# Where a two-layer transformer kernel splits its expert weights: spread over four stages in place of one

## The reference, cut to what matters

```python
def _attention(h, W_qkv, b_qkv, W_proj, b_proj):
    qkv = h @ W_qkv + b_qkv
    ...
    scores = jnp.einsum('blhd,bmhd->bhlm', q * scale, k)
    attn = jax.nn.softmax(scores, axis=-1)
    o = jnp.einsum('bhlm,bmhd->blhd', attn, v).reshape(b, l, c)
    return o @ W_proj + b_proj
# layer 0
h = _modulate(_layernorm(x), shift_msa, scale_msa)
x = x + gate_msa * _attention(h, W_qkv, b_qkv, W_proj, b_proj)
h = _modulate(_layernorm(x), shift_mlp, scale_mlp)
x = x + gate_mlp * (jax.nn.gelu(h @ W_fc1 + b_fc1, approximate=True) @ W_fc2 + b_fc2)
# layer 1: the same attention, then
gate_logits = xf @ w_gate
topk_logits, topk_idx = jax.lax.top_k(gate_logits, 2)
hmid = jax.nn.gelu(jnp.einsum('tc,ech->eth', xf, w1) + b1[:, None, :], approximate=True)
eo = jnp.einsum('eth,ehc->etc', hmid, w2) + b2[:, None, :]
moe = jnp.einsum('te,etc->tc', cw, eo).reshape(B, N, C)
return x + g_mlp[:, None, :] * moe
```

## Time and profile before

| | us |
|---|---|
| median of three runs | 1630.94 (1626.31 to 1634.62) |
| the profiled execution, its own time | 1625.62 |
| span of its core, first to last instruction | 1623.9 |
| mean granted TensorE clock | 0.922 of full speed |

### The profile page before, as it was taken

One profiled execution on the slowest core, in us unless ns is written; L12 is line 12 of the kernel. 1 busy time (PEld: TensorE's weight loads), 2 busy tenths in 40 slices (PEclk: granted clock), 3 DMA queues, 4 the chain that ended last, 5 costly groups with the idle time before them and its releaser, 6 DMA issues. The chain is left out here.

```text
span 1623.9 us, 25041 instructions
## 1 busy us (share of the span) xinstructions
PE 1400.8 (86%) x8657; PEld 870.6 (54%) x8657; DVE 1092.9 (67%) x1859; ACT 798.2 (49%) x1537; POOL 647.2 (40%) x873
## 2 busy tenths in 40 slices
PE   4787988998899879987789899999977299999995
PEld 2563333333333458976633333333325299999995
DVE  3657878887797254446489889889926556656663
ACT  0441766766677552225327677677763233333331
POOL 0125767767720000001269999995004612112121
PEclk9995989998899989998859999999998599999998
DMA  7275577657720309003660222220019466767673
GB/s 187 63 201 99 137 190 166 179 174 174 178 90 3 136 10 292 1 1 95 187 103 11 47 46 46 46 47 3 3 61 356 145 204 189 238 189 236 187 234 77
DMA packets 93396, 204.22 MB, mean 126 GB/s; under 512 B 35846, under 2 KB 61384, under 8 KB 90028
## 3 DMA queue, kind: packets, MB, share of 16 engines
q1 hardware_dynamic: 59788, 121.26, 23.4%
q0 software_dynamic: 33488, 81.41, 22.5%
HBM read 131.56 MB, written 72.12 MB: 125 GB/s over the span
## 5 line engine op out<-in xcount | busy, mean ns | idle before, releaser
L958 DVE TENSOR_REDUCE att_neg_max<-att_for_max 128x1 f32<-128x1024 f32 x512 | 601.7, 1220 | 106.5 <-PE att_for_max L1033 103.8
L943 ACT ACTIVATE att_probs<-att_scores 128x512 f32<-128x512 f32 x1002 | 523.9, 606 | 262.3 <-PE att_scores L1072 261.8
L1083 PE MATMUL att_out<-att_probs,V 128*32 128x512 f32 x2048 | 283.9, 627 | 3.9 <-ACT att_probs L943 2.0
L1072 PE MATMUL att_scores<-att_QS,att_KS 56*128 56x512 f32 x618 | 235.1, 467 | 38.1 <-DMA att_QS<-att_neg_max_rows 21.2
L1033 PE MATMUL att_for_max<-att_KS,att_QS 54*128 54x512 f32 x640 | 247.8, 474 | 0.7 <-DVE att_neg_max L958 0.5
L1072 PEld LDWEIGHTS att_scores<-att_QS,att_KS 56*128 56x128 f32 x618 | 105.4, 192 | 205.1 <-ACT att_probs L943 140.9
L1033 PE MATMUL att_for_max<-KS,QS 54*128 54x512 f32 x384 | 165.9, 535 | 25.8 <-DVE att_neg_max L958 13.1
L1875 ACT ACTIVATE experts_gelu<-experts_proj,experts_b 128x256 f32<-128x256 f32 x171 | 81.3, 475 | 208.6 <-PE experts_proj L1944 185.4
L1944 PE MATMUL experts_proj<-experts_x_parts,w_parts 128*128 128x256 f32 (+1 forms) x1197 | 174.1, 286 | 1.4 <-DVE experts_x_parts L1669 1.4
L1823 POOL DMA_INDIRECT sums_of_experts<-experts_y,experts_rows x38 | 61.3, 1613 | 260.0 <-DVE experts_y L1705 254.2
L1072 PE MATMUL att_scores<-QS,KS 56*128 56x512 f32 x384 | 150.7, 466 | 12.2 <-ACT att_probs L943 10.7
(11 more groups left out here) (227 smaller groups left out, 2004.9 us busy)
## 6 DMA issues: line engine op xcount, KB each, us to landing
w_parts<-w_parts SPq DMA_DIRECT2D x20, 2304.0 KB, 8.7
w_parts<-att_w_parts POOLq DMA_DIRECT2D x15, 864.0 KB, 5.9
w_parts<-w_parts SPq DMA_DIRECT2D x5, 2592.0 KB, 15.6
qk_halves<-qkv_qk_parts SPq DMA_DIRECT2D x40, 288.0 KB
w_parts<-att_w_parts POOLq DMA_DIRECT2D x20, 576.0 KB, 5.6
slot_rows<-mlp_blank_rows SPq DMA_DIRECT2D x2, 5145.0 KB, 28.2
att_QS<-qk_halves POOLq DMA_DIRECT2D x120, 72.0 KB
att_KS<-qk_halves POOLq DMA_DIRECT2D x60, 144.0 KB
```

What stands on the lines that cost most here:

```text
L943: nc.scalar.activation(PR[st % 2][:, j, :], score_bank(st, n), ACT.Exp, scale=SCALE).then_inc(exp_done, 1)
L958: nc.vector.tensor_reduce(negm[half][:, c:c + 1], psM[ring % 2][:].rearrange("p a n -> p (a n)"), AX_X, ALU.max, negate=True).then_inc(rin ...
L1072: nc.tensor.matmul(score_bank(st, n), KS[g % SLOTS][rows, p, k * P:(k + 1) * P], QS[g % SLOTS][rows, half, p, :], start=True, stop=True).t ...
L1083: last = nc.tensor.matmul(psO[32 * j:32 * j + 32, :], T.V[:, g, k, 32 * j:32 * j + 32], PR[st % 2][:, j, :], start=(k == 0), stop=(k == KT ...
```

## The change

The list of 30 pieces is dealt out: 6 to qkv 0 (3 before POOL's wait for the stores of q and k, 3 behind `load_group`), 8 to attention 0 (one per half of a group, from group 2 on, for four groups), 10 to MLP 0 (one at each 3.6 units), 6 to qkv 1 (as in qkv 0). The code of a piece is the same, moved into a class. In the qkv stages the parts' buffers lie in the unused part of the output tile `heads_out`, and in MLP 0 in buffers of their own. The blank rows leave MLP 0 and are written in attention 1 by POOL's queue, in six shares, one behind each load of a group. `router_rows` moves ahead of the load of group 2.

```diff
+class Splitter:
+    def load(self, pool):
...
+    def split(self, pool):
...
+    def finish(self, pool):
+        for slot, done in enumerate(self.piece_out):
+            if self.outs[slot]:
+                pool.wait_ge(done, 16 * self.outs[slot])
...
 # qkv_stage, POOL
+            S.load(pool)
             v = T.V[:].rearrange("p g k (j d) -> p (g k j) d", j=HG)
...
             pool.wait_ge(v_filled, 4)
+            for _ in range(len(pieces) // 2):
+                S.split(pool)
             for c in range(QK_CHUNKS):
...
             load_group(pool, T, 0, T.QS0, T.KS0, group_in)
+            for _ in range(len(pieces) - len(pieces) // 2):
+                S.split(pool)
+            S.finish(pool)
             pool.wait_ge(group_in, LOADS)
 # attention_stage, POOL
+            def blank_rows(n):
+                rows = T.slots.rearrange("(k t p) r -> t p k r", t=ETILES, p=P)
+                k0, k1 = n * BLOCKS // LATER, (n + 1) * BLOCKS // LATER
+                for t in range(ETILES):
+                    nc.gpsimd.dma_start(rows[t][:, k0:k1, :], blank[:, t:t + 1, :].broadcast_to([P, k1 - k0, ROW])
+                                        ).then_inc(blank_out, 16)
...
             def side_work(g):
-                for n in range((g - SLOTS + 1) * per_group, min((g - SLOTS + 2) * per_group, side)):
-                    if splits:
-                        split_piece(n)
-                    else:
-                        router_columns(n)
+                n = g - SLOTS + 1
+                if pieces:
+                    for half in range(HALVES):
+                        if half:
+                            pool.wait_ge(scores_ready, ((g - SLOTS + 1) * HALVES + half) * KT * HG)
+                        for _ in range(n * HALVES + half, len(pieces), LATER * HALVES):
+                            S.split(pool)
+                    return
+                blank_rows(n)
+                items = TILES + B * GPB
+                for m in range(n * items // LATER, (n + 1) * items // LATER):
+                    router_columns(m)
...
+                if g == 1 and not pieces:
+                    router_rows()
 # mlp_stage
-            sp.wait_ge(blank_ready, 1)
-            for t in range(ETILES):
-                sp.dma_start(T.slots.rearrange("(k t p) r -> t p k r", t=ETILES, p=P)[t],
-                             blank[:, t:t + 1, :].broadcast_to([P, SLOT_ROWS // EBLK, ROW])).then_inc(blank_out, 16)
...
+            S.load(pool)
+            for n in range(len(pieces)):
+                if n:
+                    pool.wait_ge(h_ready, n * NBLK * NF // len(pieces))
+                S.split(pool)
+            S.finish(pool)
 # program
-                qkv_stage(nc, T, l, W)
-                attention_stage(nc, T, l, W, splits if l == 0 else [])
+                qkv_stage(nc, T, l, W, splits[24:30] if l else splits[0:6])
+                attention_stage(nc, T, l, W, [] if l else splits[6:14])
-                mlp_stage(nc, T, l, W, layers[1])
+                mlp_stage(nc, T, l, W, splits[14:24], layers[1])
```

More of the change, by code:

```diff
@@ L488, in qkv_stage @@
         stored = [sem(f"stored{c}") for c in range(QK_CHUNKS)]
-        pieces = [len(chunk_pieces(c)) for c in range(QK_CHUNKS)]
+        stores = [len(chunk_pieces(c)) for c in range(QK_CHUNKS)]
         def hT_of(i):
@@ L533, in _ @@
             for c in range(QK_CHUNKS):
-                act.sem_inc(stored[c], 16 * pieces[c])
+                act.sem_inc(stored[c], 16 * stores[c])
             norm_root(nc, act, N, 0)
@@ L709, in attention_stage @@
         last = sb("last_inverse", [P, BLK], F32)
[L710 to L712 removed]
+        if pieces:
+            S = Splitter(nc, T, pieces, sb("w_f32", [P, FF], F32), [sb(f"w_parts{n}", [P, 2, FF], F32R) for n in range(2)],
+                         sem)
         else:
+            blank = sb("blank_rows", [P, ETILES, ROW], F32)
             wgate = sb("w_gate_rows", [P, C, E], F32)
@@ L925, in _ @@
             pool.wait_ge(wp_gated, B)
-            for n in range(2):
-                if splits:
-                    pool.wait_ge(piece_out[n], 16 * outs[n])
+            if pieces:
+                S.finish(pool)
+            else:
+                pool.wait_ge(blank_out, 16 * (ETILES * LATER + 1))
         @block.scalar
@@ L1237, in mlp_stage @@
         hp = [sb(f"hidden_parts{n}", [P, 2, BLK], F32R) for n in range(RING)]
-        blank = sb("blank_rows", [P, ETILES, ROW], F32)
+        S = Splitter(nc, T, pieces, sb("w_f32", [P, FF], F32), [sb(f"w_parts{n}", [P, 2, FF], F32R) for n in range(2)], sem)
         YB = TPB + 1
```

146 lines of the change are left out of this document (77 added, 69 removed).

## The result

The changed kernel took 1651.5 us (median of 4 runs, 1646.8 to 1656.2) against 1632.5 before: a ratio of 1.0136, interval 1.0102 to 1.0171. It is 1.4% slower; the prediction said 1619 with a range of 1602 to 1638.

What follows compares the result with a forecast made beforehand. Attention 0 was held to lose time as maxima wait behind group loads, then to a lowered clock; MLP 0 PE-bound, qkv a chain over all engines. Terms -30 + 17 + 1 + 0 = -12 gave 1619 us, range 1602 to 1638.

Steps and rivals of the forecast that it cites:

- the two qkv stages: qkv 0 and 1: six pieces each add 8.5 us a stage, 17 for both, bounds 8 and 36.
- The path: qkv stages: three pieces behind the load reach the barrier, next stage at 131.3 against 127.3, +4.0 us.
- The period of 7.44: Time from cast to next cast of a piece, in us, used twice for the pieces behind the qkv load.
- sharing: qkv stages: pieces share DMA engines with the last stores and `load_group`, 1.5 us a stage, bounds 0 and 8.
- rival B: qkv stages: late loads pace the pieces, 19.5 us a stage, 39 for both; total +10, 1641 us; chance 0.17.
- The start: qkv stages' start: POOL's pieces block DVE, 3 us a stage, bounds 0 and 6.
- The rule cited from the Trainium skill: VectorE contends with GpSimd reading SBUF if it has two SBUF inputs, or casts or scales in a two-port mode.
- Attention 0: Fewer pieces leave POOL no backlog, so loads start some 4 us ahead of spans: gain of 30 us, bounds 14 and 41.
- Rival A: Attention 0 only reaches attention 1's level, -20 to -25.4 us; total 1624 to 1629; chance 0.27, shared with another rival.
- The rule of turns: Each DMA engine takes packets from its queues by turns, so fewer pieces help less than fewer loads would.
- MLP 0: Ten pieces may hold casts and subtractions, mostly covered: +1 us, bounds 0 and 4.
- Attention 1: Blank rows behind each load and earlier router rows: some collisions go, others come, 0 us, bounds -8 and +10.

Runs made afterwards that it cites:

- e1: The change with only the three pieces ahead of `load_group` in each qkv stage, none behind, and 14 in attention 0: 1611.1 us, ratio 0.9892.
- e2: The change with no pieces in the qkv stages and 20 in attention 0: 1612.1 us, ratio 0.9889.
- e11: e8 plus three casts and subtractions of a full piece behind POOL's fills in each qkv stage, no further DMA: 1630.5 us, ratio 1.0010.
- e12: e8 plus three piece loads and five writes in each qkv stage, paced by the first q/k parts, no arithmetic: 1613.7 us, ratio 0.9903.
- e13: Kernel before, with its 30 pieces spaced evenly over attention 0's half groups and router rows made ahead of group 2: 1629.5 us, ratio 0.9998.
- e4: The change with the blank rows written in MLP 0 by SP again: 1640.6 us, ratio 1.0071.
- e8: e2 with the blank rows written in MLP 0 by SP again: 1605.5 us, ratio 0.9867.
- e3: The change with all three loads for the pieces behind `load_group` issued ahead of it, two into extra buffers: 1651.8 us, ratio 1.0134.
- e5: e1 plus three casts and subtractions of a piece's size behind `load_group`, without loads or writes: 1618.6 us, ratio 0.9939.
- e9: e8 with attention 0's first piece waiting for span 1's maxima: 1604.4 us, ratio 0.9867.

## Why the prediction was wrong

The step that failed is **the two qkv stages**: "Sum 4.0 + 3 + 1.5 = 8.5 a stage, 17 for both" measured 22.0 and 18.6, 40.6 for both. The path was the right one, since POOL's last write does end the stage. The terms on it were too small: it was to end at 131.3 and ended at 149.2. Of these 17.9 us, 7.3 are `load_group`, issued by 112.8 in place of 105.5; 10.3 are the two periods between casts, 25.2 in place of 14.9; and 0.3 the write and the step to the next stage, 7.2 in place of 6.9. The period of 7.44 came from attention 0; here, with the engines 0.87 to 1.04 busy from 110 to 135, it was 10.5 and 14.7. The term for this was sharing, 1.5 with bounds 0 and 8. With the 4.0 it stands for the three pieces behind the load, and these cost 17.0 and 16.7 (e1). What it left out is that the pieces also delay the stores of q and k (9.3 and 10.2 us), so that the stage would have grown even without POOL's chain behind them.

The warning could have been had from the kernel before. Its windows of the end of qkv 0, the share of the engines second from the end:

```profile
105.00:110.00 5.00, 4.49 (x22) 3.53 (x21) 3.45 (x6) 1.05 (x2) 0.52 (x1) 1.00 0.91 230
110.00:115.00 5.00, 5.00 (x26) 3.84 (x25) 1.12 (x2) 1.01 (x2) 0.00 (x0) 1.00 0.74 261
115.00:120.00 5.00, 3.11 (x24) 2.87 (x23) 3.07 (x6) 1.37 (x2) 0.00 (x0) 1.00 0.70 231
120.00:125.00 5.00, 0.37 (x3) 0.13 (x2) 0.46 (x1) 0.00 (x0) 0.00 (x0) 0.86 0.66 206
```

From 105 to 125 these leave some 5 us of free engine time. Three pieces are 4.0 MB, and at the 297 to 352 GB/s of the change's windows from 120 to 135 they take 11 to 13 us (an estimate from these rows): 6 to 8 us more than there is room for. "Most stores are out by then", as rival B's text says against it, was wrong.

- **The start**: 3 with bounds 0 and 6 was 4.0 us by DVE's timeline, and 5.7 and 4.2 at the stage's end (e1 against e2); the held subtraction (2.3) was foreseen, the 2.4 of L344 were not. The rule cited from the Trainium skill, "SBUF — State Buffer", section "Who interferes with whom", agrees in both its halves: the subtractions with two SBUF inputs were held (3.35 us in e11), and so was L344, a scaling. The transfers ahead of the load, which I had at nothing, cost 8.3 and 5.5 where they stand alone (e12, with 2.4 for L344 in it).
- **Attention 0**: -30 was right for its spans (327.1 to 300.4, forecast 297; mean of five alike by OZ 295.4 against 324.3). Its loads start where I had put them, some 4 us ahead of a span (229.2 against 233.6, 280.3 against 284.7). The stage as a whole gained 20.4, in the mean of the five 25, since its first part lost 3 to 6: a collision of the kind that I had described, at a place that I had not looked at, and a lower clock. The mechanism (fewer pieces, no backlog, loads on time) is supported by e13, where the backlog, the late loads and the loss all stay (PE waits 20.9 us for the maxima's rows), but no run changes the loads' time alone. Rival A's half gain does not hold. The rule of turns that it cites, the Trainium skill's "DMA: Bandwidth & Descriptors", section "Queues, rings and completion order", is not tested by any run here.
- **MLP 0**: +1, measured 1.1. **Attention 1**: 0, bounds -8 and +10, measured +6.4 in this profile; in the mean the kernels with blank rows there have 7.0 more than those without. The blank rows are a cost, while in MLP 0 they cost at most 1 us (122.8 against e4's 121.9, e2's 122.5 against e8's 123.5).
- **Rival B** had the sign right, and 19.5 a stage against 22.0 and 18.6; both windows passed 97, my sign for it. The late loads, its mechanism, are in the trace (waits of 5.6 and 10.0 us), but they are not the whole cause: with the loads in time the stages keep 100.1 and 100.9 (e3), since SP's stores then end them. So that its sum comes so near is partly luck.

Attention 0's first part differs by up to 9 us between kernels with the same code there (78.6 in e1, 87.9 in e5). What differs is PE's busy time, by 8.5 us for the same instructions, and its granted clock:

```profile
132.38:211.00 78.62, 71.10 (x318) 30.13 (x318) 68.67 (x67) 37.77 (x72) 53.46 (x67) 0.78 0.56 124
129.93:217.80 87.87, 79.56 (x318) 32.37 (x318) 70.98 (x67) 37.91 (x71) 54.64 (x68) 0.68 0.53 123
```

e1 spends 35.2 us of it at 1.2 GHz, e5 55.4. Over all twenty kernels each further us at 1.2 GHz goes with 0.5 us of length (a line through the twenty, correlation 0.94).

Open: why the clock rises sooner or falls again in one of these kernels and not in the other, and why mending the first part in e9 is paid back later, could not be settled from one profile per kernel. It is also open whether the pieces delay the stores by their bytes, by the engines' time that their packets take, or by the turns of the queues. What part of the blank rows' cost is the clock, what POOL's router work, was not taken apart.

## What to carry to other kernels

Before work with transfers is moved into an idle engine's gap, add up the time that the transfers need on the DMA engines and what the engines have free toward the stage's end: a piece's period was 7.44 us in one stage and 10.5 and 14.7 in another. And ask for two ends, that of the moved chain and that of the stores that it delays. Idle time of the queue that issues says nothing of room in the engines that carry it. Try a change's parts alone: here fewer pieces in attention 0 and ten in MLP 0 gained 1.3%, the pieces in the qkv stages and the blank rows in attention 1 cost more than that.
